# Eight pairs of batches through three layers on one core: for pairs four to eight the cross product in two column tiles, with the sums of codes on GpSimd

## The reference, cut to what matters

```python
x = x + matmul(fake_quant(layernorm(x), s1, z1), fake_quant(ctx, s2, z2))   # layer 1, per batch
x = x + attention(layernorm(x))      # qkv_w, 32 heads of 32, rope, causal, softmax, out_w
x = x + ffn(layernorm(x))            # W plus 16 low-rank updates
# fake_quant: q = clip(round(v / s + z), 0, 255); returns (q - z) * s
```

## Time and profile before

| | |
|---|---|
| median of 3 runs | 621.9 us (621.54 to 622.08) |
| span of the profiled execution | 620.4 us |
| PE, DVE, ACT, POOL busy | 97%, 76%, 47%, 2% |
| TensorE clock granted | nine tenths or more in all 40 slices |
| one trip of the middle loop | 58.2 us |

### The profile page before, as it was taken

How to read it: one execution, slowest core, us unless ns; L and a number is a source line. 1 busy time by engine, 2 the same in 40 slices (tenths; PEclk the granted TensorE clock), 3 DMA queues, 4 the chain that set the end, 5 groups by cost and what they waited for, 6 DMA issues and landing times.

```text
span 620.4 us, 12885 instructions
## 1 busy us (share of the span) xinstructions
PE 601.3 (97%) x4937; PEld 310.6 (50%) x4937; DVE 472.8 (76%) x938; ACT 292.3 (47%) x366; POOL 11.5 (2%) x17
## 2 busy tenths in 40 slices
PE   3898999999999999999999999999999999999998
PEld 1463454455455545554555455545545554454455
DVE  6899998788659965987596769659964789867661
ACT  5887695865464546534644554464431243110010
POOL 3000010000000000000000000000000000000000
PEclk9999999999999999999999999999999999999999
DMA  8999995861464175226712671464241042232311
GB/s 319 387 386 361 388 365 205 277 208 69 165 220 161 69 254 193 95 81 258 266 71 97 207 237 68 161 217 130 102 136 35 1 172 102 85 119 85 114 55 53
DMA packets 38912, 108.14 MB, mean 174 GB/s; under 512 B 3802, under 2 KB 4186, under 8 KB 38880
## 3 DMA queue, kind: packets, MB, share of 16 engines
q1 hardware_dynamic: 37744, 104.35, 47.5%
q0 software_dynamic: 992, 3.18, 1.5%
q10 hardware_dynamic: 144, 0.18, 0.2%
HBM read 99.30 MB, written 8.39 MB: 174 GB/s over the span
## 4 chain that ended last, share of the span: by engine, by line
PE 84%; DVE 5%; SPq 4%; DMA 4%; ACT 1%; issue 1%; ACTq 0%; DVEq 0%
PE dense L1259 16%; PE dense L1261 16%; PE dense L1260 16%; PE cross L1308 7%; PE turn L1250 6%; PE dense L1426 4%; PE dense L1427 4%; PE dense L1428 4%; DVE wq L860 4%; PE score L1387 2%; SPq L600 2%; DMA wq<-in_qkv_w 2%; PE score L1413 2%; DMA raw<-in_ctx 2%; PE dense L1442 1%; PE cross L1473 1%
## 5 line engine op out<-in xcount | busy, mean ns | idle before, releaser
L1259 PE MATMUL dense<-wq,xn_h 128*128 128x512 f16 x400 | 151.9, 380 | 0.0
L1260 PE MATMUL dense<-wq,xn_h 128*128 128x512 f16 x400 | 151.6, 379 | 0.0
L1261 PE MATMUL dense<-wq,xn_l 128*128 128x512 f16 x400 | 151.6, 379 | 0.0
L351 ACT ACTIVATE code<-raw,cst,qc 128x1024 uint8<-128x1024 f32 x72 | 87.7, 1235 | 6.7 <-DMA raw<-in_ctx 6.5
L1308 PE MATMUL cross<-code,q1t 128*128 128x512 f16 x256 | 73.4, 387 | 3.0 <-DVE xa L867 1.4
L1261 PEld LDWEIGHTS dense<-wq,xn_l 128*128 128x128 f16 x400 | 39.1, 98 | 47.2
L1259 PEld LDWEIGHTS dense<-wq,xn_h 128*128 128x128 f16 x400 | 39.1, 98 | 41.5 <-issue 1.6
L1260 PEld LDWEIGHTS dense<-wq,xn_h 128*128 128x128 f16 x400 | 39.2, 98 | 38.2
L351 ACT ACTIVATE code<-lnt,cst,qc 128x1024 uint8<-128x1024 f32 x32 | 39.6, 1239 | 28.4 <-DMA lnt<-in_ctx 25.4
L906 DVE SCALAR_TENSOR_TENSOR at<-cst,score 128x512 f32<-128x512 f16 x24 | 16.4, 683 | 37.4 <-PE score L1387 37.2
L1426 PE MATMUL dense<-wo,rope 128*128 128x512 f16 x112 | 42.5, 379 | 0.0
(11 more groups left out here) (204 smaller groups left out, 992.6 us busy)
## 6 DMA issues: line engine op xcount, KB each, us to landing
raw<-in_ctx SPq DMA_DIRECT2D x72, 512.0 KB, 4.5
lnt<-in_ctx SPq DMA_DIRECT2D x32, 512.0 KB, 4.2
wo<-in_ctx SPq DMA_DIRECT2D x16, 512.0 KB, 8.6
wo<-in_qkv_w SPq DMA_DIRECT2D x12, 512.0 KB, 11.7
wq<-in_qkv_w SPq DMA_DIRECT2D x8, 512.0 KB, 11.9
x_scratch<-xa SPq DMA_DIRECT2D x8, 512.0 KB, 3.0
wq<-x_scratch SPq DMA_DIRECT2D x8, 512.0 KB, 3.7
wq<-in_ctx SPq DMA_DIRECT2D x7, 512.0 KB, 11.7
```

What stands on the lines that cost most here:

```text
L351: act.activation(low_bytes, src, ACT.Identity, scale=qc[:, 1:2], bias=z2).then_inc(s_u8, 1)
L1259: pe.matmul(bank[:, :], a_h[:, k, :], w_hi, start=(k == 0 and not started), stop=False)
L1260: pe.matmul(bank[:, :], a_h[:, k, :], w_lo, start=False, stop=False)
L1261: ins = pe.matmul(bank[:, :], a_l[:, k, :], w_hi, start=False, stop=(k == KC - 1 and not last))
```

## The change

For pairs 3 to 7 (`TILED = 3`; "four to eight" counted from one) the cross product is done differently; pairs 0 to 2 keep the old form.

- `cross` replaces `chunk`. Its stationary operand is only the 64 columns of row codes of one batch. The result of batch b goes to partitions 64b to 64b+63, so two products of the two batches use the two column halves of the array, one after the other in the list. There are 32 of them a pair, in four groups of eight. A group covers four chunks, and chunks now alternate between the batches.
- GpSimd adds the codes of each batch (`add_codes`): as 32-bit words that hold two codes, two additions of 256 words a chunk, from a start value that takes the fixed high bytes away. DVE turns the sums to f16 (`sums_as_f16`), and `cross_shift` adds them to the result by eight products of 512 columns, whose stationary operand is `128 - z1` in two f16 parts.
- `tiled_evac` (two instructions of 128x512) takes the place of the four of 64x1024. The constant of the rows changes accordingly; the new constants are made by five small DVE instructions in the first pair.
- The ring has eight places (`RING = 8`), and an ACT quantise also waits for GpSimd's addition of the chunk eight before it.
- The rows of the pair after next are fetched from ACT's queue, after `exponent(i, 0)`, where GpSimd did it.
- The groups stand at other places than the chunks did.

```diff
-RAW, RING = 2, 6
+CODE_SUM = -0x20032000
+TILED = 3
+RAW, RING = 2, 8
@@ scalar, quantise
-                taken = CHUNKS * i + c - (CHUNKS % RING - 1 if c < CHUNKS % RING else RING - 1)
+                taken = CHUNKS * i + c - (RING - 1)
                 if above(taken):
                     act.wait_ge(s_cmm, taken)
+                if tiled(i) and not (isinstance(i, int) and i == TILED and c < RING):
+                    act.wait_ge(s_acc, taken - CHUNKS * (TILED - 1))
@@ scalar
+            def rows_after_next(i):
+                act.wait_ge(s_sc, 4 * i + 2)
+                act.wait_ge(s_xs, i + 2)
+                act.dma_start(x_early, x_pair[i + 2, :, :]).then_inc(s_xr, 16)
@@ scalar, next_pair
-                q(10, 11)
+                q(10)
+                if late:
+                    q(11)
                 exponent(i, 0)
-                q(12)
+                if not isinstance(i, int) or i < PAIRS - 2:
+                    rows_after_next(i)
+                q(12 if late else 11)
                 exponent(i, 1)
                 qk_evac(i, 2)
+                if not late:
+                    q(12)
                 q(13)
@@ gpsimd
+            def add_codes(i, c):
+                pool.wait_ge(s_u8, CHUNKS * i + c + 1)
+                if c < 2:
+                    pool.wait_ge(s_cbank, 2 * (i - TILED) + 1)
+                else:
+                    pool.wait_ge(s_acc, CHUNKS * (i - TILED + 1) + c - 1)
+                words, sums = code[:, c % RING, :].bitcast(I32), acc_words[:, c % 2, :]
+                half = NT // 2
+                for h in range(2):
+                    cols = slice(h * half, (h + 1) * half)
+                    ins = pool.tensor_tensor(sums[:, cols], words[:, cols], acc_from.to_broadcast([P, half]) if c < 2 else sums[:, cols], ALU.add)
+                ins.then_inc(s_acc, 1)
@@ vector
+            def sums_as_f16(i):
+                dve.wait_ge(s_acc, CHUNKS * (i - TILED + 2))
+                dve.tensor_copy(acc[:, :], acc[:, :].bitcast(U16T)).then_inc(s_accf, 1)
+
+            def tiled_evac(i, n):
+                dve.wait_ge(s_cbank, 2 * (i - TILED) + 2 + n)
+                cols = slice(n * NT, (n + 1) * NT)
+                dve.scalar_tensor_tensor(x_rows(i)[:, cols], X[n][:, :], step, x_rows(i)[:, cols], ALU.mult, ALU.add).then_inc(s_ce, 1)
@@ vector, next_pair
-                cross_evac(i + 1, 0)
+                if late:
+                    cross_evac(i + 1, 0)
...
                     softmax_out(i, 2)
+                    sums_as_f16(i + 1)
                     softmax_out(i, 3)
-                    cross_evac(i + 1, 1)
+                    tiled_evac(i + 1, 0)
+                    tiled_evac(i + 1, 1)
                     c_low(i, 0)
                     v_sum(i, 1)
@@ tensor
+            def cross(i, *ks):
+                for kc in ks:
...
+                    pe.wait_ge(s_u8, CHUNKS * i + 2 * kc + 2)
+                    for n in range(2):
+                        for b in range(2):
+                            ins = pe.matmul(X[n][b * SEQ:(b + 1) * SEQ, :], q1t[:, kc, b, 0, :],
+                                            code[:, (2 * kc + b) % RING, n * NT:(n + 1) * NT], start=(kc == 0), stop=False)
+                            if n:
+                                ins.then_inc(s_cmm, 1)
+
+            def cross_shift(i):
+                pe.wait_ge(s_shift, 1)
+                pe.wait_ge(s_accf, i - TILED + 1)
+                for n in range(2):
+                    for part in range(2):
+                        for b in range(2):
+                            ins = pe.matmul(X[n][b * SEQ:(b + 1) * SEQ, :], shift[:, part:part + 1].to_broadcast([P, SEQ]),
+                                            acc_sums[:, b, n * NT:(n + 1) * NT], start=False, stop=(part == 1))
+                    ins.then_inc(s_cbank, 1)
@@ tensor, next_pair (t and shifted call cross and cross_shift of pair i + 1)
-                    qkv(i, 1, {2: [at(codes)], 5: [at(codes_turned, 0), at(qk_turn, i, 0), at(m, 0)], 6: [at(c, 0)], 7: [at(c, 1)]})
-                    qkv(i, 2, {0: [at(c, 2)], 1: [at(c, 3)], 2: [at(c, 4)], 3: [at(codes_turned, 1), at(qk_turn, i, 1)], 4: [at(c, 5), at(m, 1)], 6: [at(middle_biases, i), at(scores, i, 0)], 7: [at(c, 6)]})
-                qkv(i, 3, {1: [at(c, 7)], 2: [at(m, 2)], 6: [at(turned, i, 1), at(qk_turn, i, 2)]})
-                if isinstance(i, int) and i == 1:
+                    qkv(i, 1, {3: [at(codes)], 5: [at(m, 0)], 6: [at(codes_turned, 0), at(qk_turn, i, 0)]})
+                    qkv(i, 2, {1: [at(t, 0, 1)], 3: [at(codes_turned, 1), at(qk_turn, i, 1)], 4: [at(m, 1)], 6: [at(middle_biases, i), at(scores, i, 0)], 7: [at(t, 2, 3)]})
+                late = isinstance(i, int) and i == 1
+                if late:
+                    qkv(i, 3, {1: [at(c, 7)], 6: [at(turned, i, 1), at(qk_turn, i, 2)]})
                     qkv(i, 4, {1: [at(turned, i, 2), at(p_turn, i, 0)], 3: [at(p_turn, i, 1)], 4: [at(evacuated, i, 1), at(qk_turn, i, 3)], 6: [at(scores, i, 1)], 7: [at(c, 8, 9)]})
-                elif ahead:
-                    qkv(i, 4, {1: [at(turned, i, 2), at(p_turn, i, 0)], 4: [at(qk_turn, i, 3)], 6: [at(scores, i, 1)], 7: [at(p_turn, i, 1), at(c, 8, 9)]})
-                else:
-                    qkv(i, 4, {1: [at(turned, i, 2), at(p_turn, i, 0), at(m, 3)], 4: [at(qk_turn, i, 3)], 6: [at(scores, i, 1)], 7: [at(p_turn, i, 1)]})
-                qkv(i, 5, {1: [at(c, 10, 11), at(m, 4)], 2: [at(c, 12, 13), at(m, 5)], 3: [at(c, 14, 15), at(values_due, i, 0)], 4: [at(values, i, 0)],
-                           6: [at(evacuated, i, 0), at(p_turn, i, 2)], 7: [at(p_turn, i, 3)]})
+                    qkv(i, 5, {1: [at(c, 10, 11)], 2: [at(c, 12, 13)], 3: [at(c, 14, 15), at(values_due, i, 0)], 4: [at(values, i, 0)],
+                               6: [at(evacuated, i, 0), at(p_turn, i, 2)], 7: [at(p_turn, i, 3)]})
+                else:
+                    qkv(i, 3, {2: [at(m, 2)], 5: [at(t, 4, 5)], 6: [at(turned, i, 1), at(qk_turn, i, 2)]})
+                    if ahead:
+                        qkv(i, 4, {1: [at(turned, i, 2), at(p_turn, i, 0)], 4: [at(qk_turn, i, 3)], 6: [at(scores, i, 1)], 7: [at(p_turn, i, 1)]})
+                    else:
+                        qkv(i, 4, {1: [at(turned, i, 2), at(p_turn, i, 0), at(m, 3)], 4: [at(qk_turn, i, 3)], 6: [at(scores, i, 1)], 7: [at(p_turn, i, 1)]})
+                    qkv(i, 5, {0: [at(t, 6, 7)], 1: [at(m, 4)], 2: [at(m, 5)], 3: [at(values_due, i, 0)], 4: [at(values, i, 0)],
+                               6: [at(shifted), at(evacuated, i, 0), at(p_turn, i, 2)], 7: [at(p_turn, i, 3)]})
```

More of the change, by code:

```diff
@@ L97, in build @@
         lw = sb("lw", [P, 2, 2], F32)
+        acc = sb("acc", [P, 2 * DM], F16)
         qkt = at[:, 0:2 * DM].rearrange("p (j c) -> p j c", j=4)
@@ L123, in build @@
         d16 = pr[:, 0, :].bitcast(F16)
+        acc_words = acc[:, :].bitcast(I32).rearrange("p (b n) -> p b n", b=2)
+        acc_sums = acc[:, :].rearrange("p (b n) -> p b n", b=2)
+        shift = lw[:, 0, 0:1].bitcast(F16)
+        acc_from = lw[:, 0, 1:2].bitcast(I32)
+        tiled_const, step = lw[:, 1, 0:1], lw[:, 1, 1:2]
         s1, z1 = cst[:, C_SCAL:C_SCAL + 1], cst[:, C_SCAL + 1:C_SCAL + 2]
@@ L184, in build @@
         s_cmm = sem("s_cmm")
+        s_xr = sem("s_xr")
+        s_acc = sem("s_acc")
+        s_accf = sem("s_accf")
+        s_shift = sem("s_shift")
         s_clast = sem("s_clast")
@@ L255, in bias_by_vector, with tiled, block_of @@
             return not isinstance(i, int) or i > 1
+        def tiled(i):
+            return not isinstance(i, int) or i >= TILED
+        def block_of(i, c):
+            return (c % 2, c // 2) if tiled(i) else (c // KC, c % KC)
         def above(value):
@@ L621, in load_chunk @@
                     sp.wait_ge(s_u8, CHUNKS * i - (0 if c == 0 else 2))
[L622 removed]
+                b, kc = block_of(i, c)
+                sp.dma_start(slots[n], ctx_v[i, b, kc, :, :]).then_inc(s_slot[n], 16)
             def load_weight(j):
@@ L674, in next_set @@
                     load_chunk(i + 2, 1)
-            with sp.Fori(1, PAIRS - 2) as i:
+            next_set(1, True)
+            with sp.Fori(2, PAIRS - 2) as i:
                 next_set(i, True)
@@ L747, in _ @@
             pool.tensor_tensor(xa[:, :], xa[:, :], outb[:, :], ALU.add).then_inc(s_cp, 1)
-            with pool.Fori(1, PAIRS - 2) as i:
-                rows_after_next(i)
+            pool.wait_ge(s_shift, 1)
+            pool.memset(acc_from, CODE_SUM).then_inc(s_acc, CHUNKS)
+            pool.wait_ge(s_acc, CHUNKS)
+            with pool.Fori(TILED, PAIRS) as i:
+                for c in range(CHUNKS):
+                    add_codes(i, c)
             pool.wait_ge(s_st, 16 * PAIRS)
@@ L813, in row_codes @@
                 dve.wait_ge(s_a, i + 1)
-                link(dve.tensor_scalar(rs1[:, :], rs1[:, :], qc[:, 3:4], qc[:, 4:5], ALU.mult, ALU.add))
```

(12 more changed lines are left out.)

20 lines of the change are left out of this document (13 added, 7 removed).

## The result

| | before | after |
|---|---|---|
| median | 621.92 us (621.54 to 622.08, 4 runs) | 635.93 us (632.41 to 636.04, 4 runs) |
| span of the profiled execution (its time) | 620.4 us | 634.2 us (636.04 us) |
| PE, DVE, ACT, POOL busy | 97%, 76%, 47%, 2% | 95%, 74%, 46%, 20% |
| mean granted clock of TensorE | 1.00 | 0.986 |
| one trip of the middle loop | 58.24 to 58.25 us | 60.95 to 61.37 us |

The ratio is 1.0215, with a 95% interval of 1.0198 to 1.0231: the changed kernel is 14 us slower. The forecast was slower, by 5.6 us (627.5). The direction was right and the time lies inside the range (617 to 637), but the change of the time is two and a half times what was forecast.

What follows compares the result with a forecast made beforehand. PE's dense instruction list bounds the kernel. Span 620.4 + 4.3 (five trips, wait less column saving) + 1.0 (tail) + 0.3 (first pair) = 626.0; with 1.5 for the median, 627.5 us; 8 in 10: 617 to 637.

Steps and rivals of the forecast that it cites:

- columns and switches: PE's cross product and shift: column halves run together, 5.31 instead of 6.90 us a pair with switches, -1.6 us.
- wait for chunk 15: Last cross group: PE asks at +3.37 us, ACT's quantise ends at +5.76, so PE waits 2.45 us a trip.
- tail (`c_low`): Evacuation follows the shift products and `c_low` follows it, late for the projection: +0.2 us a pair, +1.0 in all.
- rival D: The 2.5 us wait lowers PE's clock, costing 2 us more each: +10, 637 us; chance 0.13 together with (C).
- (C): GpSimd's additions slow DVE in the normalisation and row codes: +9, 636.5 us; chance 0.13 together with rival D.
- the first pair: Five small DVE instructions of about 0.19 us before the two half codes, mostly covered by a DVE wait: +0.3 us.
- (B): Column halves of the cross product take turns, 9.62 instead of 6.90 us: +24.8, 646.7 us; chance 0.09.
- rival (A): PE's wait for chunk 15 is absent or under a microsecond, so the columns decide: -6.7, 615.2 us; chance 0.16.

Runs made afterwards that it cites:

- the last run: Changed kernel with ACT's codes 14 and 15 before the copy of the second probability tile, `v_sum` early and `c_low` ahead of the evacuations: 614.64 us, ratio 0.9889.
- the run with the wait filled: Changed kernel plus 26 unused products of 192 columns on PE between the halves of the last cross group: 628.25 us, ratio 1.0107.
- the run with the codes first: Changed kernel with ACT quantising chunks 14 and 15 before it copies the second turned probability tile: 617.40 us, ratio 0.9927.

## Why the prediction was wrong, and where it was right

With the last run there is a trip without any wait, and the terms can be put beside their measured sizes, in us per trip:

| term | forecast | measured | by |
|---|---|---|---|
| columns and switches | -1.6 | -1.4 | 56.70 against 58.10 (58.25 less the 0.15 lost before the projection) |
| wait for chunk 15 | +2.45 | +2.47 | the gap in the PE timeline |
| tail (`c_low`) | +0.2 | +0.17 | 0.76 against 0.59 us from turn to projection |
| fall of the clock | 0, as rival D +2 | +1.65 | trips with and without it, one execution |
| sum | 59.2 | 61.1 | 58.25 - 1.4 + 2.47 + 0.17 + 1.65 = 61.1 |

**The step that failed** is the choice to leave the clock out of the sum, rival (D), which the prediction named with a price of 2 us a wait and gave, together with (C), 0.13. The forecast took "it is 1.00 throughout" as a property of the loop, while it is a property of a list without gaps; the one piece of evidence on gaps, the low clock after the idle start, spoke for D and was named without being given weight. It is in the trace of before, where two products of 512 columns last 1.06 us together at first and 0.59 from 20.11 us on:

```profile
18.90 1.06 PE L1308 MATMUL cross<-code,q1t 128*128 128x512 f16 x2
...
20.11 0.59 PE L1308 MATMUL cross<-code,q1t 128*128 128x512 f16 x2
```

What the runs showed in its place is a second loss behind each wait, 1.65 us. Five falls of 1.65 us are 8.2 us. The forecast span of 626.0 and these 8.2 make 634.2, which is the span that was measured; the agreement to a tenth is luck. The columns gave back 0.2 us a trip less than forecast, 1 us in all, and the stretch before the loop, for which the first pair had put +0.3, was 0.9 us shorter in the profiled execution than before. The run with the wait filled shows the same from the other side, with a span of 626.5.

**The columns** were right in kind and 0.2 us a trip too good. The halves of the array run at the same time, so (B) is out: eight products and both switches take 1.085 us of the list (in the run with the codes first the product ahead starts at 259.52, so they could start at 259.735, and the next product starts at 260.82), 0.22 more than four pitches, against the 0.20 taken from the bias rows. The two products of a pair start 3 to 4 ns apart. Five such groups make 5.43 us against 6.90, which is -1.5; the trips say -1.4.

The Trainium skill ("TensorEngine Tiling (Array Packing)", Key Properties and Restrictions) says that changing the tiling mode drains the engine and that a column tile loses the fast weight load. By the first, the trace agrees: 0.22 us a group, both ways together. For the second the trace agrees too: the loads of 64 columns last 0.109 us each (160 of them, from 0.106 to 0.156), longer than those of 128 columns in the full form (0.098). But it costs almost nothing here, since two such loads just fit a pair's pitch: the pairs follow one another after 0.24, 0.216 and 0.216 us.

**The tail** came out as forecast, but not as read: `c_low` was not just in time before (328.06 to 328.20), it already cost 0.15 us.

**The wait for chunk 15** came where and as long as counted. But the reading of ACT's 2.98 us of idle time, that it "can't be used", was an error: it held for the order of the list, not for the data, and moving two instructions up was worth 18.5 us of median. As rival (A) put it, the columns would then decide. They do, with 617.4 us against A's 615.2; the difference is mostly the columns' 0.2 us and the 0.25 us for `v_sum`, five times each.

**GpSimd (C)**: the additions follow one another after 0.68 us (forecast 0.68), and DVE's instructions beside them do last longer, by 0.26 to 0.35 us each in the ten seen of one line. None of it reaches PE in the changed kernel: with and without the additions' work the trips are the same, 59.45 us without a fall and near 61.1 with one, and chunk 15 is ready 5.76 us after the scores as before. The slack was enough, then; C's delay is real and would count where the chain is tight.

**The range** held the time only because it reached for D at its upper end; with the fall in the sum the single number is 635.7.

## What to carry to other kernels

Where an edit takes time out of a dense list, look for the producer that is now due sooner, and then at its engine's list for what stands ahead of it without feeding it: here two quantises behind a copy and an exponential turned a gain of 4.5 us into a loss of 14. Price a wait of the matrix engine in two parts, its length and what its clock does afterwards, and take the second from any idle stretch in the trace that shows it. After a move, ask what the moved work had been covering; the wait for the value sum appeared only because the last group no longer stood in front of it, and the one for `c_low` grew because the evacuation in front of it now waits for the shift products, which stand later in PE's list.

## What the runs showed of the hardware

- TensorE's clock fell to the lower level after an idle time of 2.47 us (shown as 2.27) in an otherwise dense list, behind five of five such waits in one execution and three of five in another, and not behind 20 waits shown as 1.62 us. The fall came from 0.3 us before the end of the wait to 0.9 us behind it, and the clock came back by itself after about 3 us of products. A fall cost 1.65 us where trips with and without it stand in one execution; the changed kernel's own trips are 1.5 to 1.9 us over 59.45. The time of the changed kernel's executions went with their mean clock: the one of 632.41 us had 0.991, the three near 636 had 0.986 to 0.987. What decides whether a wait of 2.47 us makes it fall is open.
- Filling the idle time with 26 useless products kept the clock up, at no cost in PE's time. That is a repair where a producer can't be made faster; it was worth 7.7 us here.
- Two products in the two column halves, with 64 stationary columns each, run at the same time: the two start 3 to 4 ns apart, and eight take 0.99 us of the list up to the next start (1.085 with the switch in front) where eight full ones take 1.72.
- The load of 64 stationary columns in that form takes 0.109 us, that of 128 in the full form 0.098.
- A GpSimd addition of 256 int32 words in 128 partitions is shown as 0.73 us in the median (up to 1.18) and the next follows after 0.68, where DVE is shown with 0.69 us for 512 fp32 words. A DVE instruction with two such inputs that starts beside an addition lasts 0.95 to 1.04 us.
- The idle time printed before a product is 0.15 to 0.2 us short of what PE loses (2.27 for 2.47, 0.33 for 0.48), and at the projection a loss of 0.15 us isn't printed at all.
